# One TensorE branch behind the last expert sums, softmax scaling by head, fewer final transfers, and three weight loads without their wait

## The chip, the cores and the metric

The kernel runs on one core of one Trainium2 chip. The metric is the device time of one execution in microseconds. A core has the engines TensorE (PE; its weight loads are told as PEld), VectorE (DVE), ScalarE (ACT), GpSimd (POOL) and SyncE (SP), and 16 DMA engines that all issuers share.

## The reference, cut to what matters

```
x = x + 0.5 * ffn(layernorm(x))
x = x + attention(layernorm(x))
x = x + 0.5 * ffn(layernorm(x))
```

x is 8 batches of 256 tokens of 256 features, float32. The `ffn` is a mixture of 64 experts, 8 for each token and at most 32 tokens for each expert: a softmax over the router's logits, `h = silu(xg @ w1.T) * (xg @ v1.T)`, `y = h @ w2.T`, and each token gets the weighted sum of its experts' rows. The attention has 16 heads of 128 in 4 groups that share keys and values: `softmax(q k.T / sqrt(128)) v`, then the output projection.

## The kernel before, in words

The work runs in three stages: expert layer 0, the attention in four blocks of two batches, and expert layer 1. The program writes every engine's queue out by hand, and semaphores order them.

**Expert layer** (`expert_layer` in each engine's block). After the router, VectorE picks the tokens of every expert (lines 916 to 938), TensorE spreads the result over the partitions (line 1372), and VectorE writes slot tokens and indices (line 943). GpSimd then gathers the rows of 128 slots, one gather for each of the 16 groups of four experts (line 548), from a table in DRAM that SP wrote (`store_table`). A ring of six buffers `slots` holds them. `slot_step` is a software pipeline over the groups: transpose the gathered slots (line 1192), up product (1273), `gate` on ScalarE (588), `hidden` on VectorE (876), its transpose (1264), down product (1283), the high part of the weighted result on ScalarE (592) and the low part on VectorE (882). `sum_slots` adds three groups behind: TensorE multiplies with one-hot marks and sums into PSUM banks 6 and 7, in layer 1 also bank 5 (lines 1204 and 1220). `sum_slots` of a group waits for VectorE's low part (`down_free`). `keep_busy` issues products that nobody reads (line 1228).

An expert takes its first 32 tokens, so only early tokens are reached, and the sums cover the first 512 (layer 0) or 640 (layer 1). Whether a later one is used is known from `limit`, a number that VectorE writes in step 0 and that TensorE loads into a register behind the last sums (line 1388). A branch (line 1390) skips the code for further ranges, which isn't run with these inputs. In layer 0 stand 14 products of `keep_busy` in front of that load. Behind the branch comes the attention: its first work is the transposes of the normalised tiles `xn4`, which VectorE writes (line 1058).

**Weight loads.** SP loads the weights of each group in order of the groups into homes in SBUF, of which 12 are there at once. In layer 1 it loads groups 0 to 6 during the attention, 7 and 8 when the attention is done, then stores the table, then waits until the first four gathers have landed (`wait_for_gathers`, line 435), and loads groups 9 to 11. Layer 0 has no such wait. Groups 12 to 15 wait for a home to come free.

**Attention step.** One step is two heads of one batch; a block has 16. In step n TensorE issues the scores of step n+1, transposes the probabilities of step n (line 1487), and does projections, the output product of step n-1 and the product with the values (`three`, lines 1431 to 1433: high and low parts as three products). VectorE takes the maxima (1084), ScalarE the exponentials (736), VectorE scales them: it waits for all four, takes the reciprocals of the row sums (1090) and multiplies the four 128x256 parts (1092), two for each head, and one semaphore `probs_ready` tells TensorE. The transposed probabilities are split in a high part (744) and a low part (1119), and so is the result `o` (719 and 1070). In the last block's last steps there are no projections to fill the queue. Behind step 15's transposes TensorE does the first transposes of layer 1 (1299).

**The end.** Behind the last sums VectorE and ScalarE copy the banks to `stage` (lines 964, 679, 966), and three engines issue the transfers to `out`: four wide ones of 128 KB (`store_wide`, line 369) and eight narrow ones of 16 KB (`store_narrow`, line 373). SP waits for all of them at the end (line 482); line 77 is the end of the program, where every engine drains.

```
                for s in range(GROUPS - 2, GROUPS):
                    sum_slots(layer, s)

                if layer == 0:
                    keep_busy(14)
                pe.wait_ge(limit_ready, layer + 1)
                most = nc.tensor.value_load(limit[0:1, 0:1], min_val=0, max_val=T)

                with nc.tensor.If(most >= FIRST[layer]):
```

## Time and profile before

| what | us |
|---|---|
| three runs | 660.22, 656.1, 654.06 |
| median | 656.1 |
| the profiled execution | 656.69 |
| its span, first to last instruction | 654.6 |
| TensorE busy | 622.7 |
| VectorE busy | 503.5 |
| ScalarE busy | 382.4 |
| GpSimd busy | 61.7 |

The span is what the trace shows; the execution takes 2.1 us more around it. All times in the rows are counted from the span's start. A timeline row gives start, duration, engine, line, operation and tiles; xN stands for N instructions in a row, and the bracket gives the idle time before and what ended it. A q behind an engine is its sequencer, which issues, waits and branches. Layer 0 takes about the first 90 us, the attention lasts to about 568, and layer 1 is the rest.

### The profile page before, as it was taken

Reading aid. Unit: us, or ns where it says so; the run is one execution under the profiler, and the core shown is the slowest. Engines: PE = TensorE matmul, PEld = TensorE weight load, DVE = VectorE, ACT = ScalarE, POOL = GpSimd, SP = SyncE. Lnnn points to the kernel's source line nnn. Section 1 sums busy time; section 2 is a strip of 40 time slices with the busy share of each in tenths; the row PEclk is TensorE's granted clock in tenths of the full one; section 3 lists DMA queues with packets and bytes.
Section 4 is the critical chain, followed back from the end, with each engine's and each line's share of the span. In section 5 each row is a group of like instructions: output and inputs, shape, how many; then the busy total and the mean of one; then the engine's idle time right before and its main releaser. Section 6 shows DMA issues by size and latency. Waiting matters only on the chain.

```text
span 654.6 us, 12253 instructions
## 1 busy us (share of the span) xinstructions
PE 622.7 (95%) x4604; PEld 539.4 (82%) x4604; DVE 503.5 (77%) x1316; ACT 382.4 (58%) x1040; POOL 61.7 (9%) x83
## 2 busy tenths in 40 slices
PE   8599989999999999999999999999999998997995
PEld 6377777999888899999889999989899997766774
DVE  6836668889997877889777788877788888684663
ACT  5724466667666656665665656666566565561442
POOL 3343000000000000000000000000000002344310
PEclk9789989999999999999999999999999999999999
DMA  8999870000000000000000000000000009675881
GB/s 314 339 412 421 308 263 1 2 1 1 1 2 1 1 2 1 2 0 2 1 2 1 2 0 1 2 2 1 1 2 1 1 1 380 248 251 183 312 317 43
DMA packets 27620, 62.52 MB, mean 96 GB/s; under 512 B 7014, under 2 KB 17382, under 8 KB 27558
## 3 DMA queue, kind: packets, MB, share of 16 engines
q1 hardware_dynamic: 25398, 55.97, 22.7%
q0 software_dynamic: 1664, 5.30, 2.2%
q8 instruction: 39, 0.64, 0.4%
q10 hardware_dynamic: 496, 0.43, 0.3%
q14 instruction: 23, 0.19, 0.1%
HBM read 54.34 MB, written 7.34 MB: 94 GB/s over the span
## 4 chain that ended last, share of the span: by engine, by line
PE 83%; DVE 11%; ACT 2%; DMA 2%; issue 1%; another core or an unknown queue 0%; POOL 0%; POOLq 0%; SPq 0%; DVEq 0%; ACTq 0%
PE bank L1431 20%; PE bank L1433 19%; PE bank L1432 19%; PE bank L1487 8%; PE bank L1220 4%; PE bank L1273 4%; PE bank L1283 2%; PE bank L1192 2%; PE bank L1228 1%; DVE ln L824 1%; DVE probsT_lo L1119 1%; DVE negmax L1084 1%; DMA slots<-token_table,slot_index 1%; DVE struck L902 1%; PE bank L1299 1%
## 5 line engine op out<-in xcount | busy, mean ns | idle before, releaser
L736 ACT ACTIVATE probs<-bank,negmax 128x256 f32<-128x256 f32 x256 | 121.4, 494 | 0.9 <-DVE negmax L1084 0.9
L744 ACT CAST probsT_hi<-bank 128x512 fp32r<-128x512 f32 x128 | 68.7, 590 | 70.7 <-PE bank L1487 70.7
L719 ACT ACTIVATE o_hi<-bank,bv 128x512 fp32r<-128x512 f32 x64 | 44.2, 690 | 66.7 <-PE bank L1433 66.7
L1119 DVE TENSOR_TENSOR probsT_lo<-bank,probsT_hi 128x512 fp32r<-128x512 f32 x128 | 81.9, 681 | 0.7 <-ACT probsT_hi L744 0.7
L1084 DVE TENSOR_REDUCE negmax<-bank 128x2 f32<-128x512 f32 x128 | 81.7, 680 | 0.0
L1092 DVE TENSOR_SCALAR probs<-probs,rowinv 128x256 f32<-128x256 f32 x256 | 73.5, 351 | 2.3
L1431 PE MATMUL bank<-wo_hi,o_hi 128*128 128x256 f32 x256 | 73.1, 285 | 0.0
L1433 PE MATMUL bank<-wo_hi,o_lo 128*128 128x256 f32 x256 | 72.6, 284 | 0.0
L1432 PE MATMUL bank<-wo_lo,o_hi 128*128 128x256 f32 x256 | 72.3, 282 | 0.0
L1070 DVE SCALAR_TENSOR_TENSOR o_lo<-bank,bv,o_hi 128x512 fp32r<-128x512 f32 x64 | 48.0, 750 | 28.4 <-ACT o_hi L719 28.3
L1487 PE MATMUL bank<-ident,probs 128*128 128x128 f32 x512 | 66.4, 273 | 0.9 <-DVE probs L1092 0.9
L1487 PEld LDWEIGHTS bank<-ident,probs 128*128 128x128 f32 x512 | 57.3, 140 | 1.3 <-DVE probs L1092 1.3
L736 ACT ACTIVATION_READ_ACCUMULATOR probs<-bank,negmax 128x1 f32 x256 | 57.8, 226 | 0.0
L558 POOL TENSOR_SCALAR early_xn<-x,ln 128x256 f32<-128x256 f32 x8 | 9.8, 1235 | 483.5 <-DVE ln L854 483.5
L1431 PE MATMUL bank<-xT_hi,wq_hi 128*128 128x512 f32 x128 | 54.4, 425 | 0.2 <-DVE k_even_lo L1070 0.2
L1431 PE MATMUL bank<-probsT_hi,v_hi 128*128 128x512 f32 x128 | 51.1, 399 | 3.3 <-DVE probsT_lo L1119 3.2
L1433 PE MATMUL bank<-xT_hi,wq_lo 128*128 128x512 f32 x128 | 50.4, 394 | 0.0
L1432 PEld LDWEIGHTS bank<-wo_lo,o_hi 128*128 128x128 f32 x256 | 48.3, 189 | 2.5
L1431 PEld LDWEIGHTS bank<-wo_hi,o_hi 128*128 128x128 f32 x256 | 48.3, 189 | 2.2
L1432 PE MATMUL bank<-probsT_lo,v_hi 128*128 128x512 f32 x128 | 50.2, 392 | 0.0
L1432 PE MATMUL bank<-xT_lo,wq_hi 128*128 128x512 f32 x128 | 50.1, 392 | 0.0
L1433 PE MATMUL bank<-probsT_hi,v_lo 128*128 128x512 f32 x128 | 50.0, 391 | 0.0
(192 smaller groups left out, 1451.4 us busy)
## 6 DMA issues: line engine op xcount, KB each, us to landing
up_r_<-up_in SPq DMA_DIRECT2D x16, 768.0 KB
down_r_<-down_in SPq DMA_DIRECT2D x14, 512.0 KB
up_q<-up_in SPq DMA_DIRECT2D x8, 768.0 KB, 8.8
up_o<-up_in SPq DMA_DIRECT2D x6, 768.0 KB
down_q<-down_in SPq DMA_DIRECT2D x8, 512.0 KB, 9.5
token_table<-xn SPq DMA_DIRECT2D x12, 256.0 KB, 2.4
down_o<-down_in SPq DMA_DIRECT2D x6, 512.0 KB
x<-x_in SPq DMA_DIRECT2D x4, 512.0 KB, 5.6
```

Source lines behind the costliest of these rows:

```text
L719: nc.scalar.activation(dst, src, ACT.Identity, bias=bias).then_inc(work_high, 1)
L736: nc.scalar.activation(probs[:, n % 2, t, :], scores_ps[head][:, qt * S:qt * S + S], ACT.Exp, bias=negmax[:, n % 2, t:t + 1], accum_out=ro ...
L744: nc.scalar.copy(probsT[0][:, head].rearrange("p c s -> p (c s)"), probsT_ps[head][:]).then_inc(probsT_high, 1)
L1070: nc.vector.scalar_tensor_tensor(lo, src, bias, hi.bitcast(f32), ALU.add, ALU.subtract).then_inc(work_taken, 1)
L1084: nc.vector.reduce_max(negmax[:, n % 2, 2 * head:2 * head + 2], scores_ps[head][:].rearrange("p (t s) -> p t s", t=2), AX.X, negate=True). ...
L1092: last = nc.vector.tensor_scalar(probs[:, n % 2, t, :], probs[:, n % 2, t, :], rowinv[:, n % 2, t:t + 1], None, ALU.mult)
L1119: nc.vector.tensor_tensor(probsT[1][:, head].rearrange("p c s -> p (c s)"), probsT_ps[head][:], probsT[0][:, head].rearrange("p c s -> p ( ...
L1220: last = mm(banks[n][:, D * pair:D * pair + D], marks[:, c:c + P], parts, start=start and pair == 0, stop=stop, skip_group_check=True)
L1431: mm(dst, w[0], m[0], start=start, stop=False, skip_group_check=shared)
L1432: mm(dst, w[0], m[1], start=False, stop=False, skip_group_check=shared)
L1433: return mm(dst, w[1], m[0], start=False, stop=stop, skip_group_check=shared)
L1487: last = nc.tensor.transpose(probsT_ps[head][:, c * S + qt * P:c * S + qt * P + P], probs[:, n % 2, 2 * head + qt, c * P:c * P + P], ident[:])
```

## The change

TensorE loads `limit` before the last two `sum_slots` in both layers; the branch stands right behind them. In layer 0 the cover is 8 products behind the branch in place of 14 in front of it.

The scaling of the probabilities tells TensorE by head: two semaphores `probs_ready`, and TensorE waits for each ahead of that head's transposes. The reciprocals have a semaphore of their own. In the last three scalings of the last block (of steps 13 to 15) ScalarE multiplies the second head's two parts, ahead of its high part of `o`.

Of the final transfers the wide ones are two in place of four, each over both banks (256 KB); SP issues one and ScalarE the other, and both wait for both copies. Of the narrow ones SP issues two, GpSimd four, ScalarE two.

In layer 1 SP's wait for the gathers is gone; groups 9 to 11 are loaded right behind the table's stores.

```diff
+        def store_wide(engine, odd):
+            engine.wait_ge(staged[0], 1)
+            engine.wait_ge(staged[1], 1)
+            engine.dma_start(result[0, 0:WIDE, odd:B:2, :],
+                             stage[WIDE * odd:WIDE * odd + WIDE, 0:2, :].rearrange("p n (b d) -> p (n b) d", b=2)).then_inc(out_stored, 16)
...
             store_table(1)
-            wait_for_gathers(1)
             for g in range(9, AHEAD):
                 load(1, g)
...
             sp.wait_ge(staged[2], 1)
-            for b in range(3):
+            for b in range(2):
                 store_narrow(sp, b)
-            sp.wait_ge(staged[1], 1)
-            store_wide(sp, 1, 0)
-            sp.wait_ge(narrow_stored, 16 * 3)
-            sp.wait_ge(out_stored, 16 * (B + 3))
+            store_wide(sp, 0)
+            sp.wait_ge(narrow_stored, 16 * 4)
+            sp.wait_ge(out_stored, 16 * (2 + B - 4 + 2))
...
             pool.wait_ge(staged[2], 1)
-            for b in range(3, 6):
+            for b in range(2, 6):
                 store_narrow(nc.gpsimd, b, narrow_stored)
...
                     nc.scalar.copy(stage[:, 0, :], bank[6][:]).then_inc(staged[0], 1)
-                    act.wait_ge(staged[0], 1)
-                    for odd in range(2):
-                        store_wide(nc.scalar, 0, odd)
-                    act.wait_ge(staged[1], 1)
-                    store_wide(nc.scalar, 1, 1)
                     act.wait_ge(staged[2], 1)
-                    for b in range(6, B):
-                        store_narrow(nc.scalar, b)
+                    store_narrow(nc.scalar, B - 2)
+                    store_wide(nc.scalar, 1)
+                    store_narrow(nc.scalar, B - 1)
...
+            def normalise_second_head(n):
+
+                act.wait_ge(rowinv_ready, inverted.now())
+                for t in (2, 3):
+                    scaled = nc.scalar.activation(probs[:, n % 2, t, :], probs[:, n % 2, t, :], ACT.Copy,
+                                                  scale=rowinv[:, n % 2, t:t + 1])
+                scaled.then_inc(probs_ready[1], 1)
...
+                if last and STEPS - KV <= n < STEPS - 1:
+                    normalise_second_head(n + 1)
                 take_high(o[0][:, n % 2, :, :], bv[:, kv:kv + 1])
...
-            def normalise_probs(n):
+            def normalise_probs(n, shared=False):
                 dve.wait_ge(exp_ready, exp_seen.add(4))
-                tie(nc.vector.reciprocal(rowinv[:, n % 2, :], rowsum[:, n % 2, :]))
-                for t in range(4):
-                    last = nc.vector.tensor_scalar(probs[:, n % 2, t, :], probs[:, n % 2, t, :],
-                                                   rowinv[:, n % 2, t:t + 1], None, ALU.mult)
-                last.then_inc(probs_ready, 1)
+                nc.vector.reciprocal(rowinv[:, n % 2, :], rowsum[:, n % 2, :]).then_inc(rowinv_ready, 1)
+                dve.wait_ge(rowinv_ready, inverted.add())
+                for head in range(1 if shared else 2):
+                    for t in (2 * head, 2 * head + 1):
+                        last = nc.vector.tensor_scalar(probs[:, n % 2, t, :], probs[:, n % 2, t, :],
+                                                       rowinv[:, n % 2, t:t + 1], None, ALU.mult)
+                    last.then_inc(probs_ready[head], 1)
...
-                    normalise_probs(n + 1)
+                    normalise_probs(n + 1, shared=last and n >= STEPS - KV)
...
+                pe.wait_ge(limit_ready, layer + 1)
+                most = nc.tensor.value_load(limit[0:1, 0:1], min_val=0, max_val=T)
                 for s in range(GROUPS - 2, GROUPS):
                     sum_slots(layer, s)
-
-                if layer == 0:
-                    keep_busy(14)
-                pe.wait_ge(limit_ready, layer + 1)
-                most = nc.tensor.value_load(limit[0:1, 0:1], min_val=0, max_val=T)
...
                                 last.then_inc(late_summed[layer], 1)
+                if layer == 0:
+                    keep_busy(8)
...
             def transpose_probs(n):
-                pe.wait_ge(probs_ready, probs_seen.add())
                 for head in range(2):
+                    pe.wait_ge(probs_ready[head], probs_seen[head].add())
                     for qt in range(2):
```

## Rows read from the trace of the kernel before

**Rows 1.** The page, clock that TensorE was granted, in tenths, 40 slices
```profile
PEclk9789989999999999999999999999999999999999
```

**Rows 2.** The page, chain that ended last, by engine
```profile
PE 83%; DVE 11%; ACT 2%; DMA 2%; issue 1%; another core or an unknown queue 0%; POOL 0%; POOLq 0%; SPq 0%; DVEq 0%; ACTq 0%
```

**Rows 3.** Waits: engine line waited for: us in total, times, longest us
```profile
ACT o_hi L719 <- PE bank L1433: 66.7, 64, 2.1
ACT gate L588 <- remote: 2.6, 1, 2.6
PE bank L1487 <- DVE probs L1092: 0.9, 1, 0.9
```

**Rows 4.** Timeline, TensorE, hand-over from layer 0
```profile
84.89 3.29 PE L1228 MATMUL bank<-router_w,ident 128*128 128x128 f32 x28
90.38 1.09 PE L1454 MATMUL bank<-ident,xn 128*128 128x128 f32 x8 [2.21 <-DVE xn L1058]
91.31 1.67 PE L1228 MATMUL bank<-router_w,ident 128*128 128x128 f32 x8
```

**Rows 5.** Timeline, VectorE, same stretch
```profile
88.31 1.38 DVE L1058 TENSOR_SCALAR xn<-x,ln 128x256 f32<-128x256 f32 x4
```

**Rows 6.** TensorE's branch, line 1390: duration min/median/max, first and last start
```profile
L1390 PEldq COMPARE_BRANCH  x2: 3450/3568/3686, 86.9 to 646.9; - x2
```

**Rows 7.** The load in front of it, line 1388, same columns
```profile
L1388 PEldq TENSOR_LOAD <-limit x2: 313/399/485, 86.0 to 646.2; - x2
```

**Rows 8.** Stretches: us, PE busy (records), PEclk, DMA share, GB/s
```profile
91.00:92.00 1.00, 1.00 (x10) 0.78 1.09 389
...
94.00:95.00 1.00, 1.00 (x4) 0.51 0.00 0
```

**Rows 9.** Timeline, all engines, the last attention step
```profile
561.17 1.41 DVE L1092 TENSOR_SCALAR probs<-probs,rowinv 128x256 f32<-128x256 f32 x4
...
561.77 0.69 ACT L719 ACTIVATE o_hi<-bank,bv 128x512 fp32r<-128x512 f32 x1 [0.85 <-PE bank L1433]
...
562.50 0.74 DVE L1070 SCALAR_TENSOR_TENSOR o_lo<-bank,bv,o_hi 128x512 fp32r<-128x512 f32 x1
...
562.64 1.09 PE L1487 MATMUL bank<-ident,probs 128*128 128x128 f32 x8 [0.90 <-DVE probs L1092]
...
564.36 0.36 PE L1431 MATMUL bank<-wo_hi,o_hi 128*128 128x256 f32 x1
```

**Rows 10.** Timeline, ScalarE, layer 1's normalised tiles
```profile
579.89 2.07 ACT L622 ACTIVATE xn<-x,ln 128x256 f32<-128x256 f32 x4
```

**Rows 11.** Timeline, VectorE, first gather and first hidden of either layer
```profile
38.05 0.22 DVE L863 TENSOR_REDUCE total<-slots 128x1 f32<-128x64 f32 x1 [5.85 <-DMA slots<-token_table,slot_index]
...
41.65 0.26 DVE L876 TENSOR_TENSOR hidden<-gate,bank 128x96 f32<-128x96 f32 x1 [2.33 <-ACT gate L588]
...
595.15 0.22 DVE L863 TENSOR_REDUCE total<-slots 128x1 f32<-128x64 f32 x1 [2.89 <-DMA slots<-token_table,slot_index]
...
601.17 0.26 DVE L876 TENSOR_TENSOR hidden<-gate,bank 128x96 f32<-128x96 f32 x1 [4.66 <-ACT gate L588]
```

**Rows 12.** Timeline, the final transfers and their issuers
```profile
647.40 1.54 POOL L373 DMA_DIRECT2D out<-stage  x3 [18.04 <-DVE stage L964]
...
647.77 2.40 ACTq L369 DMA_DIRECT2D out<-stage  x3
...
649.53 0.73 SPq L369 DMA_DIRECT2D out<-stage  x1
...
650.21 1.08 ACTq L373 DMA_DIRECT2D out<-stage  x2
```

**Rows 13.** The DMA view, issues: KB each, median us to landing
```profile
token_table<-xn SPq DMA_DIRECT2D x12, 256.0 KB, 2.4
...
out<-stage ACTq DMA_DIRECT2D x2, 16.0 KB, 2.8
```

**Rows 14.** Line 77, the end of the program, GpSimd
```profile
L77 POOLq DRAIN  x1: 4529/4529/4529, 648.3 to 648.3; - x1
```

More of the change, by code:

```diff
@@ L430, in load_when_free @@
                 load(layer, g)
-            def wait_for_gathers(layer):
-                for n in range(IN_FLIGHT - 1):
-                    sp.wait_ge(gathered[n], 16 * (layer * len(range(n, GROUPS, RING)) + 1))
             for g in range(4):
@@ L758, in step @@
                     take_fill(*job)
+                if not (last and n == 15):
+                    inverted.add()
+                if last and STEPS - KV <= n < STEPS - 1:
+                    normalise_second_head(n + 1)
                 take_high(o[0][:, n % 2, :, :], bv[:, kv:kv + 1])
```

13 lines of the change are left out of this document (6 added, 7 removed).

## The prediction

> **What bounds the kernel now.** I read the page first: TensorE is granted full clock in almost every slice [rows 1], and the chain that ended last is TensorE for 83% and VectorE for 11% [rows 2]. Then the waits, for what TensorE lacks: in the attention it waits for scaled probabilities once, for 0.9 us [rows 3], and at the hand-over from layer 0 it waits 2.21 us [rows 4]. Everything that this change touches therefore lies in four short places: the hand-over from layer 0 to the attention, the last attention step, the first gathers of layer 1 and the end. The 15 steps of a block between them are a TensorE queue without gaps, and what is saved on VectorE there is worth nothing.
>
> **Hand-over, layer 0.** The last sums end when the row of the 14 covering matmuls begins, at 84.89, and these run 3.29 us, 0.235 each [rows 4]. The first transposes of the attention begin at 90.38, though their input, the last of four normalised tiles, is done at 88.31 + 1.38 = 89.69 [rows 5]. The rest is the branch: COMPARE_BRANCH in TensorE's sequencer took 3450 and 3686 ns in its two executions, the first from 86.9 on, so until 90.33 [rows 6], 0.05 us before the first transpose. The profile names VectorE as the releaser in [rows 4]; its tile had been ready for 0.7 us. Before the branch stand the load of `limit` and its check: the loads began at 86.0 and 646.2 [rows 7], the branches at 86.9 and 646.9 [rows 6], so 0.9 and 0.7 us.
> The Trainium skill speaks against this edit: Advanced Engine Details and Errata, Control Flow Timing, gives a compare-and-branch about 108 ns. By that figure the branch costs nothing, and moving it would leave this stage alone. Its page Runtime: NRT & Kernel Launch, Instruction fetch mechanics, says that a taken branch to code that isn't held must first fetch it. The two executions above, over thirty times 108 ns, side with the second page, and the measurement decides.
> Afterwards the load and its check come ahead of sum 14, the branch right behind sum 15, and 8 covering matmuls behind the branch. The sequencer runs ahead of the engine (the branch began at 86.9, while covering matmuls ran to 88.18), so it should reach the branch as soon as the last sums are queued. They wait for VectorE's last low part and start about 1 us before 84.89; I take 84.0. With 3.5 the branch ends at 87.5, and 8 x 0.235 = 1.9 us of cover bring 89.4. Then the tile of 89.69 is what comes last: transposes follow it as they become ready, and eight of them end near 90.3 instead of 91.3. VectorE's own work isn't delayed, for the load costs sum 14 at most 0.9, which overlaps with the end of the down product before it, and sum 15 waits for VectorE anyway. That is 1.0 us. The clock is the unknown. Before, TensorE had stood idle 2.2 us, and from 1.2 us after it resumed the granted clock was 0.50, that is 1.2 GHz, for about 3.4 us: from the mean 0.78 of one microsecond to the 0.51 of the last, four in all, two of them at 0.50 [rows 8]; the 8 covering records at 91.31 took 1.67 [rows 4] instead of 0.94 (8 x 0.1175). Now it idles 84.95 to 87.5, longer but earlier, with 1.9 us of cover behind it. If the low stretch falls on the cover, it costs little; if it falls as before, it costs the same. I take -1.2. Bounds: -2.7 (no low stretch: 1.0 and 1.7, half of the 3.4) and +0.5 (all the cover and the transposes at 1.2 GHz).
> **Layer 1's last sums** get the same load in front of them, and there they are on the path. It is bounded by 0 and by the whole 0.7; sum 15 waits for VectorE behind sum 14, which swallows most. I take +0.2. The branch behind them ran 3686 ns from 646.9, until 650.6, before the end at 654.6, and stays harmless.
> **Probabilities.** One semaphore for each head lets TensorE begin with half of the scaling, which counts only where it waited, in the last step. There four scalings ran 561.17 to 562.58 on VectorE and the transposes began at 562.64, while the product before them had ended by 561.77, when ScalarE began to read it [rows 9]. With two on VectorE (0.35 each) head 0 is ready at 561.9. ScalarE does the other two: the nearest row is its 128x256 pass from SBUF to SBUF, 2.07 for 4, so 0.52 each [rows 10]; from 561.2 they end at 562.2. Eight transposes at 0.11 then end at 562.8 instead of 563.6. But ScalarE's o_hi (561.77, 0.69 us [rows 9]) is queued behind its two scalings and goes to 562.9, VectorE's o_lo of 0.74 to 563.65, and the product that needs it stood at 564.36: it can come 0.65 to 0.7 earlier. I take -0.7. Bounds: -0.9 (the whole wait) and 0. The two steps before share the scaling too; ScalarE waits for the product ahead of o_hi in every step, 66.7 us in 64 of them, so 1.04 each [rows 3], which is what two scalings take, and the transposes there come only behind the next scores. So nothing changes there; if ScalarE's wait were short, 0.2 a step would be lost.
> **Final transfers.** ScalarE issues five, from 647.77 until 651.29 [rows 12], and a 16 KB transfer lands 2.8 us after its issue [rows 13]; that ends the kernel. SP issues four until 650.26, GpSimd three until 648.94. Afterwards: ScalarE three (about 0.6 + 0.75 + 0.45), to 649.7, SP three, to 649.5 or 650, GpSimd four, to 649.5. The wide ones are 256 KB now; a 256 KB write of rows of the same size lands in 2.4 us [rows 13]. So SP's wait ends near 652.6, 1.6 earlier. But GpSimd has its own last item: its DRAIN took 4529 ns from 648.3, until 652.8 [rows 14]. With a fourth transfer (0.5 us) and 0.2 of later sums it ends near 653.5, and the last barrier took 0.2 behind it. The end moves from 654.6 to 653.7: -0.9. Bounds: -1.9 (the DRAIN doesn't grow) and 0.
> **Loads ahead of the gathers.** In layer 0 nothing holds these loads, so its first gather shows what contention costs: VectorE, done with the slot indices, waits 5.85 us for its rows there and 2.89 in layer 1, where the queues are idle [rows 11]: 2.96 us more. After the change three groups of 1.28 MB go out from 588 on; at the 389 GB/s of the loads in [rows 8] they fill the engines for 9.9 us, until the second or third gather. The first `hidden` is at 41.65 in layer 0, 9.45 behind the start of that wait at 32.20; from 592.26, where the wait of layer 1 starts, that is 601.71, and the trace has 601.17 [rows 11]: only 0.5 later, because ScalarE's first gate stood 2.6 us for something that the profile doesn't name [rows 3], and the late gather would hide in that. No matmul of layer 1 waits for a load, so earlier loads give nothing. I take +0.5. Bounds: -1.8 (the unnamed gap was of these loads and goes, and the gathers aren't slower) and +4.2 (the gap comes on top, 3.0, and TensorE, idle for 2.9 us more behind its 16 covering matmuls, gets 1.2 GHz in the first groups, 1.2).
> The Trainium skill has the same as a rule: DMA: Bandwidth & Descriptors, Issuing engines are not separate DMA queues, says that transfers of all issuers share 16 engines and interleave. It sets no price; the two gathers do.
>
> **The sum.** -1.2 + 0.2 - 0.7 - 0.9 + 0.5 = -2.1 us. The profiled execution took 656.69 (span 654.6), so 654.6; it lies 0.6 above the median of the three runs, 656.1, and these spread from 654.06 to 660.22.
>
> **Rivals.**
> 1. The gathers become a new stall (slower than before). Place: between the slot indices and the first up product of layer 1. Price up to 4.2 as above. For it: layer 0's wait of 5.85 us, and that the cover I count on is a gap nobody named. Against it: the loads are only three groups, not eight. It decides from 2.6 us on, where it eats the other gains; at its full price 656.69 - 2.6 + 4.2 = 658.3.
> 2. The clock stays up at the hand-over: -2.4 instead of -1.2, 653.4. For it: 1.9 us of cover are moved to just before the attention, and before it TensorE has been busy through the whole layer. Against it: the idle stretch grows from 2.2 to 2.5 us.
> 3. The branch isn't hidden, its 3.5 us starting only when the last sum has left the engine at 84.95: 88.4, and 1.9 of cover, 90.3. The hand-over gives 0.1 and the sum is 655.7. Against it: both branches began while matmuls still ran. This is also what the 108 ns of the skill's page would leave of the edit.
>
> **Chances.** My forecast 0.50, rival 1 0.24, rival 2 0.13, rival 3 0.13. Range 651.2 to 658.8: below, all gains at their bounds or the gap gone; above, rival 1 and a little. A measurement of this kernel tells about 1% from no change, 6.6 us. None of the cases reaches that: faster by over 1% needs below 649.5, 0.03; slower by over 1% needs above 662.7, 0.04, all of it rival 1 with the spread of the runs; within 1%, 0.93.
>
> **What would show it.** Hand-over: COMPARE_BRANCH begins near 84 and still takes about 3.5, and the first attention transpose begins before 89.8. If the branch takes a fraction of that, or starts at 85 and later, that step is wrong. Last step: the wait before the transposes of the last probabilities falls from 0.90 to about 0.2. End: GpSimd's DRAIN ends last. Gathers: the first rows are read near 598 instead of 595, and the first hidden lies near 601.6 less the 1.9 us won before; if it lies over 2 us beyond that, rival 1 has it. The time would be wrong altogether if the clock's low stretches fall elsewhere in the attention.

## The result, and the profile after

The changed kernel takes 660.02 us (median of 7 runs, 658.41 to 661.25), the kernel before, on the same chip, 655.83 (7 runs, 654.06 to 660.22). The ratio is 1.0051, 95% interval 1.0027 to 1.0074: slower by 3.3 us as the ratio gives it (4.2 between the medians), where 2.1 us less was forecast, and outside the range. The profiled execution took 660.1, its span 658.2 against 654.6.

TensorE's row at the hand-over, and its branch there (the columns of [rows 4] and [rows 6]):

```profile
83.59 2.12 PE L1227 MATMUL bank<-y_parts,onehot 128*128 128x256 f32 x16 [0.52 <-issue]
89.82 3.50 PE L1235 MATMUL bank<-router_w,ident 128*128 128x128 f32 x16 [4.10 <-issue]
93.15 1.04 PE L1460 MATMUL bank<-ident,xn 128*128 128x128 f32 x8
94.02 1.06 PE L1235 MATMUL bank<-router_w,ident 128*128 128x128 f32 x8
```
```profile
L1394 PEldq COMPARE_BRANCH  x2: 3766/4584/5403, 84.4 to 649.7; - x2
```

The sums now run in one group until 85.7 and the branch begins at 84.36 (84.4 here), 2.5 us earlier than in [rows 6]. But it takes 5403 ns, until 89.76, so it ends only 0.57 us earlier. TensorE stands idle for 4.10 us, the 8 covering matmuls come after that and take 3.50 us (8 x 0.235 = 1.9 at full clock), and the transposes begin at 93.15 against 90.38 in [rows 4]. The tile they need was begun at 88.74 (88.31 in [rows 5]). The clock in that stretch (columns of [rows 8]):

```profile
88.00:89.00 1.00, 0.00 (x0) 1.00 0.97 354
89.00:90.00 1.00, 0.18 (x1) 0.73 1.08 376
...
91.00:92.00 1.00, 1.00 (x7) 0.50 1.09 389
...
93.00:94.00 1.00, 1.00 (x11) 1.00 0.93 324
```

The low stretch, 1.2 GHz, begins before TensorE has work again and lies on the cover; it is over at 93, where that of [rows 8] still went on until 95. This is why 2.8 us of later transposes became only 1.07 us of later attention: from the first row maximum of the scores on, everything lies 1.50 us behind the trace of before, of which 0.43 were there when the tiles were normalised, and at the last step it is still 1.50.

The last attention step (columns of [rows 9]):

```profile
562.67 0.91 ACT L736 ACTIVATE probs<-probs,rowinv 128x256 f32<-128x256 f32 x2 [0.24 <-DVE rowinv L1095]
562.67 0.77 DVE L1099 TENSOR_SCALAR probs<-probs,rowinv 128x256 f32<-128x256 f32 x2
...
563.49 0.67 ACT L711 ACTIVATE o_hi<-bank,bv 128x512 fp32r<-128x512 f32 x1
...
563.50 1.09 PE L1493 MATMUL bank<-ident,probs 128*128 128x128 f32 x8 [0.28 <-DVE probs L1099]
564.19 0.75 DVE L1075 SCALAR_TENSOR_TENSOR o_lo<-bank,bv,o_hi 128x512 fp32r<-128x512 f32 x1 [0.74 <-ACT o_hi L711]
...
565.22 0.37 PE L1437 MATMUL bank<-wo_hi,o_hi 128*128 128x256 f32 x1
```

The wait in front of the transposes is 0.28 instead of 0.90, and the product with o_hi, at 564.36 in [rows 9], stands at 565.22: 1.50 behind has become 0.86. The gain is 0.64, where the forecast had 0.65 to 0.7.

Layer 1's first gather and first hidden tile (columns of [rows 11]):

```profile
599.73 0.22 DVE L868 TENSOR_REDUCE total<-slots 128x1 f32<-128x64 f32 x1 [6.13 <-DMA slots<-token_table,slot_index]
...
603.74 0.26 DVE L881 TENSOR_TENSOR hidden<-gate,bank 128x96 f32<-128x96 f32 x1 [2.68 <-ACT gate L584]
```

The first rows are read 4.58 us later than in [rows 11], their wait is 6.13 instead of 2.89. At the first hidden tile 2.57 are left, since VectorE's wait for the gate there has gone from 4.66 to 2.68; after that the distance settles at 3.5 us, until the end. The 0.9 us between the two come at the second hidden tile, which follows the first after 1.77 us in the kernel before, whose next slots were transposed by the time ScalarE went on, and after 2.71 here. The clock has a share too. Waiting for the rows TensorE worked 0.87 of the 4 us from 596 to 600, and then ran at half clock, where the kernel before stayed at full clock (columns of [rows 8], first the changed kernel, then the one before):

```profile
600.00:602.00 2.00, 1.72 (x16) 0.87 1.04 424
602.00:604.00 2.00, 2.00 (x20) 0.50 0.42 130
```
```profile
602.00:604.00 2.00, 2.00 (x33) 1.00 0.99 374
```

The first up product took 1.51 us at it; the next one, at full clock again, 0.86.

The end itself (the timeline's columns, then the DMA view from 652.6 on, then line 77; the 16 KB transfer is ScalarE's last, issued at 652.71):

```profile
650.72 0.59 ACT L675 COPY stage<-bank 128x512 f32<-128x512 f32 x1 [1.69 <-PE bank L1227]
...
651.97 0.71 ACTq L372 DMA_DIRECT2D out<-stage  x1
652.44 0.73 SPq L372 DMA_DIRECT2D out<-stage  x1
```
```profile
out<-stage ACTq DMA_DIRECT2D x1, 256.0 KB, 3.5
out<-stage SPq DMA_DIRECT2D x1, 256.0 KB, 3.5
...
out<-stage ACTq DMA_DIRECT2D x1, 16.0 KB, 5.0
```
```profile
L77 POOLq DRAIN  x1: 4980/4980/4980, 652.3 to 652.3; - x1
...
L77 SPq COMPARE_BRANCH  x1: 38/38/38, 657.8 to 657.8; - x1
```

From ScalarE's copy of the last sums to the end of the span it is 7.48 us (650.72 to 658.2), before it was 7.45 (647.15 to 654.6): the list of final transfers is shorter and nothing is gained. Both wide transfers land 3.5 us after their issue, not 2.4 as in the row of [rows 13] that I had taken, and it is SyncE's wait for the landings that ends last (its branch behind that wait at 657.8), not GpSimd's DRAIN (652.3 + 4.98 = 657.3). The landing that ends it isn't a wide one (652.44 + 3.5 = 655.9) but that of ScalarE's last 16 KB, issued behind its wide one and 5.0 us under way: 652.71 + 5.0 = 657.7.

So the trace has two losses (hand-over 1.07; gathers 2.2 when they have settled, half clock included), one gain (0.64) and one zero. Two things are not the change's: 0.43 us that the execution was late by when the tiles were normalised, and 0.47 at layer 1's slot tokens, whose wait for TensorE is 0.9 against 0.4 and varies like that in the traces of other kernels too. Together they are the 3.6 us between the spans.

### The profile page after: what moved, and what is told of

Its sections match the earlier page's. It is cut to its first block, busy times and chain, and to the rows that moved or that the text cites. A ratio compares the mean times of both kernels' runs of the same rounds, so it can differ in the third digit from the quotient of the medians.

```text
span 658.2 us, 12227 instructions
## 1 busy us (share of the span) xinstructions
PE 623.3 (95%) x4592; PEld 538.9 (82%) x4592; DVE 501.6 (76%) x1310; ACT 385.5 (59%) x1046; POOL 62.2 (9%) x84
## 4 chain that ended last, share of the span: by engine, by line
PE 84%; DVE 9%; DMA 3%; ACT 2%; issue 2%; POOL 1%; POOLq 0%; SPq 0%; DVEq 0%; ACTq 0%
PE bank L1437 20%; PE bank L1439 19%; PE bank L1438 19%; PE bank L1493 8%; PE bank L1227 5%; PE bank L1280 4%; PE bank L1290 2%; DMA slots<-token_table,slot_index 2%; PE bank L1199 2%; PE bank L1235 2%; DVE probsT_lo L1126 1%; DVE negmax L1089 1%; PE bank L1306 1%; DVE ln L829 1%; DVE struck L907 1%
## 5 line engine op out<-in xcount | busy, mean ns | idle before, releaser
L1099 DVE TENSOR_SCALAR probs<-probs,rowinv 128x256 f32<-128x256 f32 x250 | 71.7, 350 | 2.3
```

The costliest lines, as they stand in the source:

```text
L1099: last = nc.vector.tensor_scalar(probs[:, n % 2, t, :], probs[:, n % 2, t, :], rowinv[:, n % 2, t:t + 1], None, ALU.mult)
```

## The experiments

Each part was first made alone. The four ran on one chip, where the kernel before took 655.78 (median of 35 runs).

**The branch edit alone.**
```diff
+                pe.wait_ge(limit_ready, layer + 1)
+                most = nc.tensor.value_load(...)
                 for s in range(GROUPS - 2, GROUPS):
                     sum_slots(layer, s)
-                if layer == 0:
-                    keep_busy(14)
-                pe.wait_ge(...); most = nc.tensor.value_load(...)
                 with nc.tensor.If(most >= FIRST[layer]):
...
+                if layer == 0:
+                    keep_busy(8)
```


> The kernel before with the branch edit alone. In the trace of the changed kernel the first branch ran 5.4 us (84.36 to 89.76) where it had run 3.45, TensorE stood idle 4.1 us, and 8 covering matmuls at 1.2 GHz followed; the lag behind the kernel before went from 0.43 to 2.7 and settled at 1.5. Theory 1 (the cover in front of the branch was what hid it, the stall is the edit's own): about +1.1 us, branch near 5.4 again, transposes of the attention 2 to 3 us later than before. Theory 2 (a chance of that one execution; the branch is 3.5 as before): the transposes 0.5 to 1 us earlier than before and -0.5 to -1.2 us.

Measured: 658.7, ratio 1.0044 (1.0022 to 1.0066), 2.9 us slower. The branch of layer 0 took 5.93 us and TensorE idled for 4.92 in front of its cover; the profiled execution was the slowest of the twelve, 663.3. Theory 1 had the place and the length of the branch, and with 1.1 us too small a price. This edit is the larger part of the loss.

**The probabilities alone.** The semaphore for each head and ScalarE's half of the scaling, the rest as before.

> The kernel before with the scaling by head alone. Theory 1 (the forecast): -0.7 us, all of it in the last step, no change in the 63 steps before it. Theory 2 (the second wait per step costs TensorE something in every step): 0 or slower; at 10 ns a step +0.6.

Measured: 654.45, ratio 0.9987 (0.9968 to 1.0006), 0.85 us less. In its trace the last scaling begins 2.80 us ahead of the kernel before (558.37 against 561.17) and the product with o_hi 3.46 ahead (560.90 against 564.36), so the last step gains 0.66 us. The interval holds 1; the saving is read from the trace, below what the times alone resolve.

**The final transfers alone.**

> The kernel before with the new final transfers alone. Theory 1 (forecast, the end is bound by issuing): -0.9 us. Theory 2 (the end is bound by moving 640 KB in rows of 1 KB, which can now begin only when both banks are copied): 0 within 0.3, the last landing about 7.5 us behind the first stage copy as in both traces.

Measured: 655.52, ratio 0.9998 (0.9978 to 1.0017): nothing.

**The loads ahead of the gathers alone.**
```diff
-            wait_for_gathers(1)
             for g in range(9, AHEAD):
                 load(1, g)
```


> The kernel before with the three loads ahead of the gathers alone. Theory 1 (the gathers share the engines with 3.8 MB of loads): VectorE waits about 6 us for the first rows instead of 2.9, +2.5 to +3 us in all. Theory 2 (the gathers are late in the changed kernel because TensorE's low clock in 584 to 591 made the slot indices late): the wait is 3 us again and the time unchanged.

Measured: 657.11, ratio 1.0017 (0.9999 to 1.0035), 1.1 us slower. VectorE's wait for its first rows was 6.56 us, as theory 1 had it, but the price was less than half of the 2.5 to 3 us that it asked. The four add up: 2.9 - 0.85 - 0.1 + 1.1 = 3.0, and the whole change measured 3.3.

In these traces TensorE's branch has very different lengths, though only the branch edit changes the code around it; here the probabilities, the transfers, the loads, and last the branch edit:

```profile
L1406 PEldq COMPARE_BRANCH  x2: 667/852/1038, 86.4 to 645.3; - x2
```
```profile
L1387 PEldq COMPARE_BRANCH  x2: 1049/1058/1067, 86.8 to 644.4; - x2
```
```profile
L1384 PEldq COMPARE_BRANCH  x2: 2889/2928/2967, 87.3 to 647.7; - x2
```
```profile
L1387 PEldq COMPARE_BRANCH  x2: 3626/4778/5930, 84.7 to 652.7; - x2
```

With the short ones (1.0 us) the transposes begin 0.5 us behind the start of the normalised tiles and no low clock follows; with the long ones they come 1.5 and 2.1 us behind in the old order (up to 2.6 in later traces of it), and half clock can follow. The profile of before had been one of the long cases, so part of what I wanted to win there was already absent in other runs of the same kernel. From here on the experiments ask three things: what makes the branch long, what the cover in front of it does, and what the loads cost.

**No branch at all.** It leaves out TensorE's load of the largest slot count and its sums for further ranges of slots, which these inputs don't reach; the 14 covering matmuls stay.

> The kernel before without TensorE's load of the largest slot count and without the branch on it, in both layers (it leaves out TensorE's sums for further ranges of slots, which these inputs do not reach); the 14 cover matmuls stay. It puts an upper bound on everything the branch can cost. Branch theory (the duration of the branch is a wait for TensorE's next instructions, and the same late fetch holds back the last output rows): the transposes behind the hand-over come no later than before, and if the fetch is now hidden by the cover they come some 1 us earlier; at the end, the stretch from the first stage copy to the end of the span is near 6.5 us instead of 7.9; the time is 1 to 2.5 us under the kernel before, some 653.5 to 654.8. Rival (the fetch costs the same wherever it falls, the branch only shows it): the same idle time reappears in front of the first transposes or inside the cover, the end stays near 7.9, and the time is within 0.5 us of before.

Measured: 651.22 against 653.25 (29 runs of before), ratio 0.9962 (0.9947 to 0.9976), 2.5 us less by the ratio. The transposes begin at 89.51, 0.46 us behind the start of the tiles (89.05). At the end:

```profile
644.21 0.59 ACT L679 COPY stage<-bank 128x512 f32<-128x512 f32 x1 [1.65 <-PE bank L1220]
```

From here to the end of the span, 650.0, it is 5.8 us, against 7.45 before. Behind the end of TensorE's work there is still a branch open in the kernel before ([rows 6], 646.9 to 650.6); without it the end comes 1.6 us sooner after the copy. In the trace of the probabilities alone, whose second branch took only 667 ns, it is 6.1 (645.53 to 651.6). The branch costs at both places, and 2.5 us (1.6 to 3.5 by the interval) is about what an edit of it can win.

**The cover stays in front, only the load comes early.**
```diff
+                pe.wait_ge(...); most = nc.tensor.value_load(...)
                 for s in range(GROUPS - 2, GROUPS):
                     sum_slots(layer, s)
                 if layer == 0:
                     keep_busy(14)
-                pe.wait_ge(...); most = nc.tensor.value_load(...)
```


> The kernel before with the load of the largest slot count moved ahead of the last two sums, as in the change, but with the 14 cover matmuls and the branch where they were, the cover in front of the branch. Theory (the price of the change's hand-over is that the branch, 5.4 to 5.9 us of idle TensorE, has its cover behind it and not in front, so that the clock falls and the tiles wait): here the branch starts at about 86 us and ends before the normalised tiles are there (88.7 to 90.1), lasts 1 to 3 us, and the layer's transposes come at 89.5 to 90.4 against 90.38; the time is 0 to 1 us under the kernel before. Rival (the early load itself makes the branch long, because it starts before TensorE's next instructions have been fetched whatever stands in front of it): the branch lasts 4 us or more, the transposes come after 91 and the time is 1 us or more over before.

Measured: 653.11 against 653.25, ratio 0.9989 (0.9974 to 1.0005). It differs from the branch edit only in where the cover stands and how much of it there is (14 matmuls in front for 8 behind), and the 2.9 us are gone; place and amount were not varied one by one. The theory's time holds but not its account of the branch: with 4547 ns it was as long as the rival had it, and the transposes began at 91.32, past the 90.4 of the theory (the tiles of this trace are 0.7 us late, 89.01 against 88.31); the clock stayed full all the same:

```profile
85.58 3.29 PE L1228 MATMUL bank<-router_w,ident 128*128 128x128 f32 x28
91.32 1.09 PE L1454 MATMUL bank<-ident,xn 128*128 128x128 f32 x8 [2.45 <-DVE xn L1058]
92.25 1.06 PE L1228 MATMUL bank<-router_w,ident 128*128 128x128 f32 x8
```
```profile
L1390 PEldq COMPARE_BRANCH  x2: 3087/3817/4547, 86.7 to 644.6; - x2
```

**Four wide matmuls as cover, in front.** As above, with
```diff
-                    keep_busy(14)
+                    for _ in range(4):
+                        mm(bank[3][:], ident[:], token_of_column[:, 0:RANGE], start=True, stop=True)
```


> The load early as in the change; in front of layer 0's branch stand 4 cover matmuls of 512 columns in place of 14 of 128, and none behind it. TensorE's program is 10 instructions shorter between sums and branch, while the covered time is about the same (4 x 512 columns against 14 x 128). Theory (it is time for the fetch to arrive that the cover buys, and the clock that it keeps): as with 14 narrow ones, the branch ends by 90 us, the transposes come at 89.5 to 90.5 and the time is within 1 us of the kernel before, on the lower side. Rival (what counts is how many instructions TensorE has issued ahead of the branch, since that sets when the next ones are fetched): with fewer instructions in front the fetch starts later, the branch lasts over 4 us as in the changed kernel, and the time is 1 to 3 us over before.

Measured: 652.72, ratio 0.9992 (0.9977 to 1.0007). The branch took 4.62 us from 83.5 and so ended at 88.1, before the first tile was normalised; the transposes began 0.47 us behind the start of the tiles, as without a branch. The rival had the length right (over 4 us) and its consequence wrong: this long branch, which began early and had its cover in front, cost nothing at the hand-over. In three of the four later traces with this cover the branch took 5.6 to 5.7 us and ended after the first tile; the transposes began 1.3 to 1.5 us behind it, still at full clock, and were done 0.2 to 0.4 us later than here.

**Quiet queues.** The branch edit alone, and SyncE waits before the rest of wq and wo:
```diff
+            sp.wait_ge(xn4_ready, 4)
             sp.dma_start(wq_raw[:, :, G * DH:], by_column[:, :, G * DH:])...
```


> The change's branch edit alone, and SyncE's loads of the rest of wq and of wo wait until four token tiles are normalised, so that far less is moved while TensorE's branch is open. Contention theory (the branch of the changed kernel is long because its instruction fetch shares a DMA engine with these loads): the branch of layer 0 falls from 5.4 to 5.9 us to 3.7 us or less and the transposes come at 91.5 or earlier. Rival (the fetch starts late after the branch however quiet the DMA engines are, because the branch now stands before code that nobody has asked for): the branch keeps 5 us or more, and the transposes stay near 93. The attention's first weights may come later by about 1 us, which does not bear on the branch.

Measured: 2844 ns for the branch, 659.83 in all, because the attention then waits for its weights (it begins 5 us late); only the branch is to be read here. It was made again, beside a second trace of the branch edit alone on the same chip.

> The same edit as the run in which SyncE's loads of the rest of wq and of wo wait for the normalised tiles, once more, beside a second trace of the branch edit alone on the same chip. Contention theory (what is loaded while the branch is open keeps TensorE's instruction fetch back): the branch of layer 0 lasts 2.3 to 3.7 us again, at least 1.5 us less than in the run beside it. Rival (one short branch was the luck of an execution): it lasts 5 us or more, or is no shorter than in the run beside it.

> The branch edit alone, a second trace, on the chip of the run beside it. If the length of the branch of layer 0 is set by what stands around it, it is 5 to 6 us again, TensorE's clock falls to half behind it, and the transposes come 2.5 us or more later than the normalised tile; if it is the luck of an execution, it is anywhere from 1 to 4 us as with the kernel before.

The branch and the stretch in which it is open, first of the branch edit (656.48 us in all), then of the quiet version (658.81):

```profile
L1387 PEldq COMPARE_BRANCH  x2: 3766/4676/5587, 83.7 to 646.3; - x2
```
```profile
85.00:90.00 5.00, 0.70 (x3) 0.70 (x4) 3.90 (x20) 4.86 (x8) 0.00 (x0) 0.72 1.03 393
90.00:93.00 3.00, 3.00 (x16) 3.00 (x16) 0.00 (x0) 0.00 (x0) 0.00 (x0) 0.50 1.08 382
```
```profile
L1388 PEldq COMPARE_BRANCH  x2: 2547/3136/3726, 84.5 to 648.8; - x2
```
```profile
85.00:90.00 5.00, 3.54 (x26) 2.83 (x24) 4.58 (x22) 4.86 (x8) 0.00 (x0) 1.00 0.02 5
90.00:93.00 3.00, 2.87 (x19) 2.32 (x19) 1.91 (x4) 1.49 (x4) 0.00 (x0) 1.00 0.47 102
```

With the 16 DMA engines full (393 GB/s) the branch of layer 0 takes 5587 ns, with them empty (5 GB/s) 2547; the earlier pair has 5930 and 2844. Both pairs say that in the changed order the branch is 3 us shorter without the traffic. What it waits for, the DMA view says, here for the changed kernel, first the 2.9 us from the start of its branch, then the 2.5 until its end (queue and kind: packets, MB, share of 16 engines):

```profile
q1 hardware_dynamic: 256, 1.23, 102.3%
```
```profile
q1 hardware_dynamic: 568, 0.93, 100.0%
q8 instruction: 1, 0.02, 2.2%
```

One 16 KB packet of instructions is moved while the branch is open, and it begins 2.9 us after the branch; 2.5 us later the branch is over. In the kernel before it begins at 87.9 and ends its branch at 90.3: nearly the same times, though that branch began 2.5 us later. The other traces show the same when the view is narrowed to a tenth of a microsecond. In all 19 with a branch, and in both layers, the branch ends 2.35 to 2.87 us behind the start of such a packet, while its own length goes from 0.46 to 5.93 us. In the four traces with a short branch in layer 0 (1.4 us at most) the packet came 1.0 to 2.0 us ahead of the branch. The shortest, in the kernel with two loads ahead of the gathers further down, began at 86.65 and ended at 87.11, and its packet stands in the window 84.6 to 84.7:

```profile
q8 instruction: 1, 0.02, 54.9%
```

So the branch ends with that packet and not after a time of its own, and an earlier branch doesn't bring the packet earlier by as much. In the quiet runs, too, the branch ends 2.4 and 2.8 us behind it; what differs is when it begins, 0.4 us behind the branch and 0.2 ahead of it, against 3.0, 3.5 and 3.1 behind in the three traces of the changed order. That full DMA engines hold it back is what these five traces suggest, but not all there is to it: in the old order it came anywhere from 84.6 to 87.9, always with full engines. What sets its time stays open. In the trace without a branch such a packet begins at 87.7 and holds nothing back: the transposes begin 1.8 us behind it. The long cases, a packet behind the start of the branch and its end behind the packet, agree with the Trainium skill (Runtime: NRT & Kernel Launch, Instruction fetch mechanics: a taken branch to code that isn't held must fetch it first). The layer 1 branch, in front of which the edit holds nothing back, is 3.8 and 3.7 us in the second pair and 3.6 and 3.3 in the first.

**The repaired versions.** Probabilities by head with the wide cover in front, transfers and loads as before:

> The change's probabilities by head, and in place of its branch edit an early load of the largest slot count with 4 cover matmuls of 512 columns in front of the branch; loads of groups 9 to 11 wait for the gathers and the final transfers are those of before. If the two savings are independent (probabilities 0.7 to 0.9 us in the last step, alone 0.9987; the wide cover alone 0.9992), the time is 1 to 2 us under the kernel before, ratio 0.997 to 0.9985, and this is the version that beats both. Rival (the savings of single runs are the chip's spread): within 0.5 us of before, with an interval that holds 1.

Measured: 650.76 against 653.14, ratio 0.9977 (0.9956 to 0.9999). With the change's final transfers added:

> As the run beside it (probabilities by head, wide cover in front of the branch, loads that wait for the gathers), and with the change's final transfers. Theory (two wide transfers that can start only when both copies are done, 320 KB each, give back what the shorter list saves): the same time as the run beside it within 0.5 us, or up to 1 us slower, and the stretch from the stage copy to the end is no shorter. Rival (fewer transfers save their issue and wait at the end, as forecast, and the changed kernel only had a late instruction fetch in its way): 0.5 to 1 us faster than the run beside it.

Measured: 651.42, the same ratio 0.9977 (0.996 to 0.9994), and both profiled spans have 7.5 to 7.6 us from the last copy to the end (the wide transfers are 256 KB each, not 320). The final transfers are worth nothing, as their own run said. The kernel before, unchanged, ran beside these for its trace:

> The kernel before, unchanged, for a trace from the chip on which the three others of this call run. If the chip or the execution decides the 2.6 us of idle time that the trace of before has in front of ScalarE's first gate of layer 1, and the half clock at 91 to 95 us, they can be missing here with the same program; the first hidden tile of layer 1 then comes 3 us after its slots and not 6, and the transposes behind the hand-over are followed by full clock. If the program decides them, both are here as in the trace of before. The time is that of before within 0.3% either way.

Its time was 654.56. The branch was long again (3953 ns) and half clock followed, 0.50 over 91 to 93; the gap was not there:

```profile
594.82 0.22 DVE L863 TENSOR_REDUCE total<-slots 128x1 f32<-128x64 f32 x1 [2.85 <-DMA slots<-token_table,slot_index]
...
597.78 0.26 DVE L876 TENSOR_TENSOR hidden<-gate,bank 128x96 f32<-128x96 f32 x1 [1.63 <-ACT gate L588]
```

From first rows to first hidden it is 2.96 us here and 6.02 in [rows 11]: the 2.6 us in front of ScalarE's first gate, put down to "remote" in [rows 3], are no property of the program. The waits have that line in the trace of before and in the three alone runs that left the loads as they were (3.3 to 3.5 us), all beside a kernel before of 655.8; they have it in none of the runs on the four other chips, where the kernel before took 652.9 to 653.4, less by about the length of the gap. The line in the traces of the transfers alone and the probabilities alone:

```profile
ACT gate L589 <- remote: 3.3, 1, 3.3
```
```profile
ACT gate L589 <- remote: 3.4, 1, 3.4
```

**How much load ahead of the gathers is too much.** First one load, of group 9 (`load(1, 9)` ahead of `wait_for_gathers(1)`):

> The kernel before, with the load of group 9 alone ahead of the wait for the gathers; groups 10 and 11 still wait. The changed kernel has all three ahead and its first rows came 3.2 us later than they would have. Theory (the gather's rows share the DMA engines with whatever load is still being moved, so that the price is the data still in flight): with one load of the three, issued some 4 us ahead of the gather, most of it has landed, VectorE's wait for the first rows is 3 to 4 us and not 6.1, and the time is within 1 us of before. Rival (any load issued ahead of the gather holds the gather back in full): the wait is 5 us or more, and the time is 1 us or more over before.

Measured: 652.4 against 653.14, ratio 0.9988 (0.9972 to 1.0004). Then two:

> The kernel before, with the loads of groups 9 and 10 ahead of the wait for the gathers; group 11 still waits. One load ahead moved the first rows by nothing, three moved them by 3 us. Theory (what counts is the data still in flight when the gather is issued, 1.28 MB a load at some 420 GB/s, 3 us each): VectorE's wait for the first rows is 4 to 5.5 us, between the 3.0 with one and the 6.1 with three, and the time is 0 to 1 us over the kernel before. Rival (a threshold: a full queue holds the gather, or none): the wait is either about 3 or about 6 us.

Measured: 656.53 against 652.87, ratio 1.0055 (1.0035 to 1.0074), 3.6 us slower. The rows of the first gather, and the DMA engines' share in front of them, with one and with two:

```profile
593.40 0.22 DVE L864 TENSOR_REDUCE total<-slots 128x1 f32<-128x64 f32 x1 [2.98 <-DMA slots<-token_table,slot_index]
```
```profile
590.00:592.00 2.00, 2.00 (x20) 2.00 (x20) 0.35 (x2) 0.00 (x0) 1.43 (x2) 1.00 0.49 195
592.00:594.00 2.00, 2.00 (x18) 1.84 (x18) 0.53 (x3) 0.11 (x1) 1.52 (x2) 1.00 0.56 164
```
```profile
596.62 0.22 DVE L865 TENSOR_REDUCE total<-slots 128x1 f32<-128x64 f32 x1 [6.15 <-DMA slots<-token_table,slot_index]
```
```profile
590.00:592.00 2.00, 2.00 (x21) 2.00 (x19) 0.41 (x3) 0.00 (x0) 1.36 (x2) 1.00 1.02 420
592.00:594.00 2.00, 1.50 (x14) 1.31 (x12) 0.00 (x0) 0.00 (x0) 1.59 (x2) 1.00 1.02 415
594.00:596.00 2.00, 0.00 (x0) 0.00 (x0) 0.00 (x0) 0.00 (x0) 1.50 (x2) 1.00 0.93 331
```

One load is through by 591 and costs nothing. Two keep the engines full to nearly 596, and the wait is 6.15, as with three (6.13 to 6.56). My theory had the right cause and the wrong law: I expected something between 3 and 6 us, and it was the rival's "about 3 or about 6". In these traces a gather that is moved while the engines are full takes 3.2 to 3.7 us more, with two loads as with three.

**The change without its branch edit**, with the wide cover instead:

> The whole change but for its branch edit, in whose place the early load with 4 cover matmuls of 512 columns in front of the branch stands. If the parts add up as measured alone (probabilities and wide cover together 0.9977, transfers nothing, loads ahead of the gathers 1.0017), the time is within 1 us of the kernel before, ratio 0.998 to 1.0005: faster than the changed kernel by 3 to 4 us, slower than the version without the early loads by about 1 us. Rival (the early loads do harm only beside the long branch, which makes everything late): the same 0.9977 as without them.

Measured: 656.82 against 652.87, ratio 1.0063 (1.0043 to 1.0083). Neither the sum of the parts (ratio 0.998 to 1.0005) nor the rival came true: the parts don't add up with the 1.1 us of the loads as first measured. So two kernels were run once more on another chip, before at 653.36.

> The loads of groups 9 to 11 ahead of the gathers, alone, once more. Where it was measured alone first, the kernel before lost 2.6 us in front of ScalarE's first gate of layer 1 behind the gather, which a later gather hides; the traces taken since have no such gap. Theory (the gather is 3 to 4 us later either way, and the gap decides how much of it shows): if the trace has a wait of VectorE for its first rows of 6 to 6.6 us and the kernel before has no gap on this chip, the time is 3 to 4 us over before, ratio 1.0045 to 1.0065, as with two loads ahead. Rival (its price is the 1.1 us first measured, and the 3.7 us with two ahead came from something else): ratio 1.0005 to 1.003. On a chip where the kernel before has the gap, both expect the latter.

Measured: 657.58, ratio 1.0062 (1.0042 to 1.0082), 4.1 us slower. Its wait for the first rows:

```profile
597.98 0.22 DVE L857 TENSOR_REDUCE total<-slots 128x1 f32<-128x64 f32 x1 [6.29 <-DMA slots<-token_table,slot_index]
...
602.29 0.26 DVE L870 TENSOR_TENSOR hidden<-gate,bank 128x96 f32<-128x96 f32 x1 [2.98 <-ACT gate L582]
```

6.29 us against 2.85 in the trace of the unchanged kernel without the gap. Half clock followed here as well (0.54 over 598 to 600, 0.61 over 600 to 602), and in each of the other traces with two or three loads ahead. From first rows to first hidden it is 4.31 us here, against 2.96 at full clock. The loads cost about 4 us where the gap is absent, and 1.1 where it is present and the late gather hides in it. With 4 in place of 1.1 the sum for the change without its branch edit comes out at +2.6 (-1.5 for the 0.9977, +4.1), 1.5 below the 4.1 that it measured; its six runs carry an interval of 1.3 either way, and nothing was done to explain the rest.

> Probabilities by head and the wide cover in front of an early load, a second time, since its first interval reached to 0.9999. If it beats the kernel before, the ratio is 0.9955 to 0.9985 again (1 to 3 us); if the first result was the spread, it is 0.999 or more.

Measured: 651.14 against 653.36, ratio 0.9964 (0.9949 to 0.9979). Probabilities by head with an early load and four wide covering matmuls in front of the branch beat the kernel before by 1.5 and 2.4 us in two series; with the 3.3 of the changed kernel that is some 5 us to it, though these two never ran beside each other.

## Why the prediction was wrong

**Hand-over, forecast -1.2, in the trace +1.07, timed alone +2.9.** The step that failed is "With 3.5 the branch ends at 87.5". I had the start right (84.0 forecast, 84.36 measured) and took the length as a property of the branch, fixed at 3.5 us. It is a wait for a packet of instructions, and it ends 2.35 to 2.87 us behind that packet's start in every trace; with full DMA engines it was 5.4 to 5.9 us in three traces of the changed order and 2.5 to 2.8 in two with the engines empty, and in eight traces of the old order anything from 0.46 to 3.95. So it ended at 89.76 where 87.5 was forecast. The second failure is where the cover stood. Rival 3 said that the branch isn't hidden, which was right, but for another reason, a late start (it began 1.3 us before the last sum ended); and it too had 3.5 us and "The hand-over gives 0.1". Even the bound of +0.5 was passed. Behind the branch, the 8 matmuls kept TensorE busy only after the idle time that they were to bridge, and they ran at half clock in front of transposes that were ready. In front of it, 14 narrow or 4 wide ones take the loss away, as two runs show. The timed loss is larger than the 1.07 of the trace because my profile was one of the slow cases of the old order. From the start of the normalised tiles to the first row maximum it took 13.6 us there. In the eight traces of the old order this is 11.4 to 11.8 five times (branches of 0.46 to 2.9 us, full clock) and 13.6 to 14.1 three times (branches of 3.45 to 3.95 us, half clock), 12.4 on the mean; in the three of the changed order it is 14.6, 15.5 and 16.1, 15.4 on the mean. The difference of the means is 3.0 us, the timed loss 2.9. The wide cover in front gives 11.4 to 11.8 in its five traces, no branch at all 11.45.
The figure of the Trainium skill (Advanced Engine Details and Errata, Control Flow Timing, about 108 ns for a compare-and-branch) does not agree with any of these branches; the shortest of all took 455 ns.

**Layer 1's last sums, forecast +0.2.** Little, as forecast: the distance grew by 0.05 us there.

**Probabilities, forecast -0.7.** Right, mechanism and size: 0.64 in the trace, 0.66 in that of the part alone.

**Final transfers, forecast -0.9, measured 0.** The failed term is "a 256 KB write of rows of the same size lands in 2.4 us". It was a store of another tile in the middle of the kernel. Here two such stores go out 0.5 us apart, together 512 KB, and both took 3.5. The sum also left out ScalarE's last 16 KB, issued behind its wide store; it took 5.0 and lands last. The second failure is that I gave the end to GpSimd's DRAIN. What ends last are the landings, and with TensorE's branch gone these come 1.6 us earlier: "The branch ... stays harmless" was wrong for the kernel before already. That the packet of instructions shares a DMA engine with the last stores is how I read this; the runs show only that branch and late landings go together.

**Loads ahead of the gathers, forecast +0.5, measured +1.1 with the gap and about +4 without.** The reading of layer 0's first gather was right: 2.96 us more were forecast, 3.2 came (6.13 less 2.89). Right too that the first gate's gap would hide some of it. What failed is "only 0.5 later": at the first hidden tile the changed kernel was 1.2 us later by the gathers (2.57 less the 0.86 and 0.47 that came before), and 2.2 from the second on. I had taken the 9.45 us of layer 0, from the start of the wait for rows to the first hidden tile; here it was 10.14 (593.60 to 603.74). The half clock behind TensorE's idle time, 1.2 in my upper bound and nothing in the sum, is the likely difference. What I could not know from one execution is that the cover is there on one chip and not on the four others. Rival 1 had this place, and "Price up to 4.2" is what two chips show; it decided beside the branch, not alone.

**The sum.** +1.07 + 2.2 - 0.64 + 0.43 + 0.47 is 3.5 of the 3.6 us by which the profiled span is longer. The range, 651.2 to 658.8, left out the case in which hand-over and gathers go wrong together; I had treated rival 1 and rival 3 as alternatives, and the place of the one and the consequence of the other came together.

## What to carry to other kernels

A branch's duration in an engine's sequencer is a wait, not a cost: starting it earlier doesn't end it earlier by as much. Look in the trace for the packet of instructions that it waits for. Leave the work that covers it in front of it, where it is queued before the sequencer stops, and check the length over several executions before a forecast is built on one. Here a load moved ahead of a gather was free when it had landed about when the gather was issued; with the second load the whole price was due. Idle time behind such a wait has a second price, the clock. A cover that the profile can't name may not be there on the next chip.

## What the runs showed that was not expected

TensorE's branch took 0.46 to 5.93 us for the same few instructions, and each time it ended 2.35 to 2.87 us behind the start of a 16 KB packet of instructions. Idle TensorE time doesn't always bring the half clock: 2.45 us idle at full clock afterwards in one run, 2.21 us and half clock in [rows 4] and [rows 8]; what separates them stays open. A branch that is still open behind the last useful matmul delays the end of the kernel by 1.6 us. And a gap of 2.6 to 3.5 us in front of ScalarE's first gate of layer 1 is there on one chip and absent on four, its cause unknown.
